# Layer 0 writes x1 transposed, with the x tile as the stationary operand, and layers 2 and 3 take their residual from an identity in the weights

## What is computed

```
x1 = x  + (own W0 of 8, 64x64, over the POSITIONS) . x + own bias, one value per position
x2 = x1 + down( silu(gate(x1)) * up(x1) )       gate, up: 512 -> 2048, down: 2048 -> 512,
                                                each with an own rank-16 adapter (A then B)
x3 = x2 + x2 . W2^T + scaled own rank-16 adapter        512 -> 512
y  = x3 + (own W3 of 200, 64x64, over the POSITIONS) . x3
```

## Time and profile before

| | us |
|---|---|
| median of the runs | 766.19 |
| the profiled execution's own time | 767.69 |
| its span in the trace | 765.9 |
| TensorE matmuls busy | 727.8 |
| VectorE busy | 601.1 |
| ScalarE busy | 284.8 |
| GpSimd busy | 255.3 |

### The profile page before, as it was taken

The page is one execution under the profiler, slowest core; times in us unless marked ns, Lnnn a source line. Parts: engine busy times, 40 slices in busy tenths (PEclk is TensorE's granted clock), DMA queues, the critical chain, the costliest instruction groups (busy, mean ns, idle before and its releaser), DMA issues.

```text
span 765.9 us, 10652 instructions
## 1 busy us (share of the span) xinstructions
PE 727.8 (95%) x3626; PEld 606.9 (79%) x3626; DVE 601.1 (78%) x1010; ACT 284.8 (37%) x508; POOL 255.3 (33%) x489
## 2 busy tenths in 40 slices
PE   6779889999999999989899999999999999899997
PEld 4547678888888888878778888888888888788886
DVE  7975768797878778799898979787888877766675
ACT  3445523333424333434353334242434333134232
POOL 4724231515223232350327162534425231241100
PEclk9979999999999999999999999999999999999999
DMA  7366520313212121203723232221212061212112
GB/s 209 87 81 194 164 80 29 104 37 108 83 56 83 55 84 56 83 27 111 248 59 109 71 103 73 70 86 58 89 55 85 28 192 32 79 29 70 42 55 83
DMA packets 65941, 66.02 MB, mean 86 GB/s; under 512 B 31712, under 2 KB 48096, under 8 KB 65888
## 3 DMA queue, kind: packets, MB, share of 16 engines
q1 hardware_dynamic: 57248, 45.92, 19.9%
q0 software_dynamic: 7296, 19.41, 8.7%
q10 hardware_dynamic: 1344, 0.02, 0.1%
HBM read 56.94 MB, written 8.39 MB: 85 GB/s over the span
## 4 chain that ended last, share of the span: by engine, by line
PE 84%; DVE 10%; issue 2%; ACT 2%; DMA 1%; POOLq 0%; POOL 0%; ACTq 0%; DVEq 0%
PE bank L1376 36%; PE bank L1474 22%; PE bank L1384 7%; PE bank L1633 6%; PE bank L1483 4%; PE bank L1622 2%; PE bank L1326 1%; PE bank L1599 1%; PE bank L1639 1%; DVE XC L882 1%; PE bank L1650 1%; PE bank L1611 1%; DVE hid L1001 1%; PE bank L1353 1%; DVE hs L1007 1%
## 5 line engine op out<-in xcount | busy, mean ns | idle before, releaser
L1376 PE MATMUL bank<-XC,WC 128*128 128x512 f32 x1344 | 332.9, 394 | 6.7 <-DVE tmp L975 2.2
L1376 PEld LDWEIGHTS bank<-XC,WC 128*128 128x128 f32 x1344 | 245.5, 190 | 54.8 <-issue 4.7
L1474 PE MATMUL bank<-wds,hs 128*128 128x512 f32 x768 | 187.6, 394 | 6.6 <-DVE X L1017 3.3
L1474 PEld LDWEIGHTS bank<-wds,hs 128*128 128x128 f32 x768 | 142.9, 190 | 35.8 <-DVE wds L960 3.8
L398 POOL DMA_INDIRECT BR<-in_L_cond_Bu_dram,boffs x64 | 71.9, 1124 | 265.7 <-DVE BL L954 251.1
L398 POOL DMA_INDIRECT BR<-in_L_cond_Bg_dram,boffs x64 | 76.1, 1189 | 95.2 <-DVE BL L954 80.2
L620 ACT ACTIVATE hs<-hid 128x512 fp32r<-128x512 f32 x64 | 40.3, 630 | 164.4 <-DVE hid L1001 111.4
L1017 DVE TENSOR_TENSOR X<-bank,X 128x512 f32<-128x512 f32 x128 | 86.5, 686 | 17.5 <-PE bank L1474 15.3
L614 ACT ACTIVATE hid<-hid 128x512 f32<-128x512 f32 x48 | 30.4, 633 | 148.4 <-DVE hid L984 75.9
L1384 PEld LDWEIGHTS bank<-UT,BL 128*128 128x128 f32 x512 | 76.4, 190 | 10.0 <-issue 2.1
L1384 PE MATMUL bank<-UT,BL 128*128 128x256 f32 x512 | 81.9, 283 | 1.3 <-ACT hid L611 1.3
(11 more groups left out here) (152 smaller groups left out, 827.9 us busy)
## 6 DMA issues: line engine op xcount, KB each, us to landing
RW<-in_L_cond_Wg_dram SPq DMA_DIRECT2D x16, 512.0 KB, 4.4
RW<-in_L_cond_Wu_dram SPq DMA_DIRECT2D x16, 512.0 KB, 5.1
RD<-in_L_cond_Wd_dram SPq DMA_DIRECT2D x16, 512.0 KB, 3.5
out_dram<-XR SPq DMA_DIRECT2D x16, 256.0 KB, 2.0
X<-in_x_dram SPq DMA_DIRECT2D x8, 256.0 KB, 6.2
udp<-in_x_dram SPq DMA_DIRECT2D x8, 256.0 KB, 4.5
x1park<-RD SPq DMA_DIRECT2D x8, 256.0 KB, 4.2
x2park<-X SPq DMA_DIRECT2D x8, 256.0 KB, 2.5
```

The source lines that it names most:

```text
L1376: last = nc.tensor.matmul(psum[:, :], WC[:, t, left, a, k, :], XC[:, right, b, k, :], start=(first and k == 0 and n == 0), stop=(k == 1 an ...
L1474: last = nc.tensor.matmul(psD[j % 2][:, :], hs[:, f, a, j * P:(j + 1) * P], wds[:, f, b, :], start=(f == 0 and n == 0), stop=(f == 1 and n ...
```

## The change

- `layer0(p)` now makes x1 transposed: four matmuls with one of the four strided slices of the x tile (`by_feature`, every fourth float) stationary and W0 plus identity moving (128 columns), then one matmul of 40 rows that adds the bias (`ones` against `bsel`). Four PSUM banks take turns. ScalarE's `xr_copy` is the only eviction. `x1_sum`, `x1_bias`, `transposes` and `add_identity` are gone; GpSimd adds the identity as it places W0.
- VectorE builds `bsel` (`bias_table`, `biases`). At the start it combines the first weights earlier.
- x1 of the two halves has its own buffers `XA` and `XB`, feature-major; the second half is parked from `XB`. `xin` has four buffers instead of two, two of them in `RD`. `load_d(0)` waits for the last `layer0` instead of the last transposes and parks.
- `down` is transposed as well: a strided slice of `wds` stationary, `hs` moving; `evict` adds to `XA`. `lora_down` is transposed too: 12 matmuls of 256 columns per duo instead of 6 of 512.
- x2 is feature-major, so `transposes2` is gone. VectorE adds the identity to W2 (`w2_identity`, end of unit 15) and to the W3 tables (`w3_identity`, end of unit 14); `x3_sum` and `y_sum` are gone. `x3_high` and `x3_low` read the PSUM bank of layer 2, and `layer2` of the next duo waits for `x3_low`. ScalarE copies y out (`y_out`), into four buffers instead of two.
- The last stretch's orders on TensorE, VectorE and ScalarE are rewritten accordingly. The warm-up is 24 matmuls of 128 columns instead of 5 of 256 and 5 of 128.

```diff
...
-    x1park = nc.dram_tensor("x1park", (HP, P, FEAT), f32).ap()
-    x2park = nc.dram_tensor("x2park", (HP, P, FEAT), f32).ap()
+    x1park = nc.dram_tensor("x1park", (P, KT, HT), f32).ap()
+    x2park = nc.dram_tensor("x2park", (P, KT, HT), f32).ap()
...
-        XR = sb("XR", [P, KT, HT])
-        X1 = sb("X1", [P, HP, FEAT])
+        XA = sb("XA", [P, KT, HT])
+        XB = sb("XB", [P, KT, HT])
...
+        xin = [udp[:, s * FEAT:(s + 1) * FEAT] for s in range(2)] + [RD[:, s, :] for s in range(2)]
...
+        def l0_bank(p):
+            return (psD[0], psD[1], psR[0], psR[1])[p % 4]
...
+        XT = [XB[:, n, :].rearrange("p (k t) -> p k t", k=2) for n in range(4)]
...
+        xc_raw = [dict(zip((B11, B21, B22), (blocks(XA)[0], blocks(XA)[1], blocks(XA)[3]))),
+                  {B11: XB11, B21: XB21, B22: XB22, T1: XB12, T2: XB11, T3: XB12, T4: XB21}]
+        xc_raw[0].update({T1: XT[0], T2: XT[1], T3: XT[2], T4: XT[3]})
...
+        def by_feature(v):
+
+            return v.rearrange("p (o k) -> p k o", k=KT)
...
+                    if p >= HP + XIN:
+                        sp.wait_ge(s_l0, p - XIN + 1)
+                    sp.dma_start(xin[p % XIN], x_pairs[p * P:(p + 1) * P, :]).then_inc(s_xin[p % XIN], 16)
 
                 def park_x1(p):
-                    sp.wait_ge(s_x1b, p - HP + 1)
-                    sp.dma_start(x1park[p - HP, :, :], x1s[p % 2]).then_inc(s_x1st[p % 2], 16)
+                    sp.wait_ge(s_xr, p + 1)
+                    at = slice((p - HP) * P, (p - HP + 1) * P)
+                    sp.dma_start(x1park[:, :, at], XB[:, :, at]).then_inc(s_x1st, 16)
...
-                        sp.wait_ge(s_tr, PAIRS)
-                        for s in range(2):
-                            sp.wait_ge(s_x1st[s], 16 * HP // 2)
+
+                        sp.wait_ge(s_l0, PAIRS)
...
+                for p in range(HP + XIN, PAIRS):
+                    load_xin(p)
+                    if p == HP + XIN + 1:
                         load_u(1)
                 load_d(0)
+                for p in range(HP, PAIRS):
+                    park_x1(p)
...
-                        last = nc.gpsimd.tensor_copy(w0bd_of(p)[rows, rows].rearrange("p (c f) -> p c f", f=KT),
-                                                     w0tab[rows, bass.ds(cols[half], RANK), :])
+
+                        last = nc.gpsimd.tensor_tensor(w0bd_of(p)[rows, rows].rearrange("p (c f) -> p c f", f=KT),
+                                                       w0tab[rows, bass.ds(cols[half], RANK), :],
+                                                       ident[rows, rows].rearrange("p (c f) -> p c f", f=KT), ALU.add)
...
-                def x1_bias(p):
-
+                def xr_copy(p):
                     act.wait_ge(s_l0, p + 1)
-                    if p == HP:
-                        act.wait_ge(s_x1, HP)
-                    if p >= HP + 2:
-                        act.wait_ge(s_tr, p - 1)
-                        act.wait_ge(s_x1st[p % 2], 16 * ((p - HP) // 2))
-                    nc.scalar.activation(x1_of(p), psD[p % 2][:, :], ACT.Identity, bias=bias[:, p:p + 1]).then_inc(s_x1b, 1)
-
-                def xr_copy(p):
-                    act.wait_ge(s_tr, p + 1)
                     if p >= HP:
                         act.wait_ge(s_xcl, 7)
                     at = p % HP * P
-                    nc.scalar.activation(XR[:, :, at:at + P], psR[p % 2][:, :].rearrange("p (k t) -> p k t", k=KT),
+                    nc.scalar.activation(XF[p // HP][:, :, at:at + P], l0_bank(p)[:, :].rearrange("p (k t) -> p k t", k=KT),
                                          ACT.Copy).then_inc(s_xr, 1)
...
+                def x3_high(d, q):
+                    act.wait_ge(c_l2, 2 * d + q + 1)
+                    if d >= 2:
+                        act.wait_ge(c_l3, 2 * (d - 2) + q + 1)
+                    nc.scalar.activation(x3s[d % 2][q][:, 0, :], psD[q][:, :], ACT.Copy).then_inc(c_x3h, 1)
...
+                def y_out(d, q):
+                    act.wait_ge(c_l3, 2 * d + q + 1)
+                    if d >= 2:
+                        act.wait_ge(c_out[d % 2][q], 16 * (d // 2))
+                    nc.scalar.activation(y[d % 2][q], psR[q][:, :], ACT.Copy).then_inc(c_y, 1)
...
+                def w2_identity():
+                    dve.wait_ge(s_w2ld, 16)
+                    for k in range(KT):
+                        own_block = w2_raw[:, k, k * P:(k + 1) * P]
+                        last = nc.vector.tensor_tensor(own_block, own_block, ident[:, :], ALU.add)
+                    last.then_inc(s_w2i, 1)
...
-                def x1_sum(p):
-                    dve.wait_ge(s_l0, p + 1)
-                    nc.vector.scalar_tensor_tensor(out=X1[:, p, :], in0=psD[p % 2][:, :], scalar=bias[:, p:p + 1],
-                                                   in1=X1[:, p, :], op0=ALU.add, op1=ALU.add).then_inc(s_x1, 1)
...
-                    nc.vector.tensor_tensor(X1[:, j, :], psD[j % 2][:, :], X1[:, j, :], ALU.add).then_inc(s_evict, 1)
+                    sums = XA[:, j % KT, j // KT * 512:(j // KT + 1) * 512]
+                    nc.vector.tensor_tensor(sums, psD[j % 2][:, :], sums, ALU.add).then_inc(s_evict, 1)
...
+                    if unit == ALL - 2:
+                        w3_identity(0)
+                        w3_identity(1)
+                    if unit == ALL - 1:
+                        w2_identity()
...
+                bias_table()
+                biases(0)
                 gather_rows()
-                biases()
...
                 move_matrices()
                 masks()
-                x1_sum(0)
-                x1_sum(1)
-                x1_sum(2)
-                g_combine(0)
-                x1_sum(3)
                 raw_low(G, 0)
-                x1_sum(4)
-                add_identity()
-                x1_sum(5)
-                x1_sum(6)
-                x1_sum(7)
                 xc_low(0, B11)
+                xc_low(0, B21)
+                sums_low(G, 0)
...
-                def x3_sum(d, q):
-                    dve.wait_ge(c_l2, 2 * d + q + 1)
-                    dve.wait_ge(s_x2, 2 * d + q + 1)
-                    if d >= 2:
-                        dve.wait_ge(c_y, 2 * d + q - 3)
-                    nc.vector.tensor_tensor(x3[d % 2][q], psD[q][:, :], x2_of(d, q), ALU.add).then_inc(c_x3, 1)
-
-                def y_sum(d, q):
-                    dve.wait_ge(c_l3, 2 * d + q + 1)
-                    if d >= 1:
-                        dve.wait_ge(c_out[q], 16 * d)
-                    nc.vector.tensor_tensor(y[q], psR[q][:, :], x3[d % 2][q], ALU.add).then_inc(c_y, 1)
...
                 for d in range(DUOS):
                     if d + 1 < DUOS:
+                        x2_sum(d + 1, 0)
+                        x2_sum(d + 1, 1)
                         xt_low(d + 1)
-                    x3_sum(d, 0)
-                    if d + 2 < DUOS:
-                        x2_sum(d + 2, 0)
-                        x2_sum(d + 2, 1)
-                    if d + 1 == DUOS:
-                        y_sum(d - 1, 0)
-                        x3_low(d, 0)
-                    x3_sum(d, 1)
+                    x3_low(d, 0)
+                    x3_low(d, 1)
                     if d + 1 < DUOS:
                         u2_mask(d + 1)
-                        if d >= 1:
-                            y_sum(d - 1, 0)
-                        x3_low(d, 0)
-                    if d >= 1:
-                        y_sum(d - 1, 1)
-                    x3_low(d, 1)
-                y_sum(DUOS - 1, 0)
-                y_sum(DUOS - 1, 1)
+                    w3_low(d, 0)
+                    w3_low(d, 1)
...
                 def layer0(p):
+
                     pe.wait_ge(s_w0c, p + 1)
                     if p < HP:
                         pe.wait_ge(s_xload[p], 16)
                     else:
-                        pe.wait_ge(s_xin[p % 2], 16 * ((p - HP) // 2 + 1))
-                    if p >= HP + 2:
-                        pe.wait_ge(s_x1b, p - HP - 1)
-                    elif p >= 2:
-                        pe.wait_ge(s_x1, p - 1)
-                    nc.tensor.matmul(psD[p % 2][:, :], w0bd_of(p), x_of(p), start=True, stop=True).then_inc(s_l0, 1)
-
-                def transposes(p):
-                    if p < HP:
-                        pe.wait_ge(s_x1, p + 1)
-                    else:
-                        pe.wait_ge(s_x1b, p - HP + 1)
-                    if p >= 2:
-                        pe.wait_ge(s_xr, p - 1)
+                        pe.wait_ge(s_xin[p % XIN], 16 * ((p - HP) // XIN + 1))
+                    if p >= 4:
+                        pe.wait_ge(s_xr, p - 3)
                     for k in range(KT):
-                        last = nc.tensor.transpose(psR[p % 2][:, k * P:(k + 1) * P],
-                                                   x1_of(p).rearrange("t (c k) -> t k c", k=KT)[:, k, :], ident[:, :])
-                    last.then_inc(s_tr, 1)
```

(54 more changed lines are left out.)

365 lines of the change are left out of this document (166 added, 199 removed).

## The result

The changed kernel takes 793.56 us (median of 4 runs, 793.33 to 793.96), the kernel before 766.39 in the same rounds (766.14 to 767.77). The ratio is 1.0351, 95% interval 1.0333 to 1.0369. I had forecast 750.6, with a range that ends at 758.5. The profiled execution has a span of 792.1 us against 765.9.

A forecast was written before the change was run, and what follows sets the result against it. Engine-alternating waits, mostly VectorE's, bound the start; TensorE bounds unit 0 and later, with short VectorE waits. Terms -3.0 - 4.4 - 1.1 + 0.3 - 7.4 = -15.6 from the 766.19 median gave 750.6 us, range 745.5 to 758.5.

The forecast's parts named there:

- The strided weight load: `down`'s 768 strided loads: stride lengthens a load but hardly its spacing, so cost nothing; ends 0 and 31 ns each.
- Bound D: Rival: strided loads not hidden in `down`, 258 ns set the pace, 23.4 us more, 774; chance 0.08.
- B: Rival: each strided load in `down` costs its extra 8.5 ns, 6.5 us in all, 757.1; chance 0.12.
- Layer 0 at the start: Start: first two pairs at half speed, then 1.2 us each, ScalarE limits; -3.0 us, ends 0 and 5 gained.
- rival C: Half the start and unit 0 gains swallowed (4.3 us), last stretch gives 5 instead of 7.4: 757.5; chance 0.15.
- Unit 0 and its end: Unit 0: cheaper pairs -1.0, waits gone -3.4, about -4.4; its end, VectorE's idle time won, about -1.1.
- The Wd transfer: End of unit 0: Wd loaded 5 us earlier, so its 3.44 us leave the chain; about -1.1 gained.
- Units 1 to 15 and the last stretch: Units +0.3 for `w3_identity`; last stretch -7.4, mainly transposes and waits removed, with `w2_identity` +0.9 and one new wait 0.5.
- wait for `x3_low`: Last stretch: `layer2` of the next duo waits for `x3_low`, hidden; wrong if TensorE waits for it in every duo.
- Two of the signs: Prediction wrong if `down` has more than 230 ns per matmul, or a layer 0 pair costs over 1.5 us.

The follow-up runs named there:

- all_flat: Changed kernel with contiguous slices in layer 0, `down` and `lora_down` at once (wrong features in each slice): 765.08 us, 0.9975 of the kernel before.
- after_xb: Changed kernel with only ScalarE's `idx_b` and `scal` transfers issued ahead of the bias wait and transfers: 792.06 us, 1.0337 of the kernel before.
- contig_warm_xb: contig plus 20 warm-up matmuls of 512 columns, x tiles 6 and 7 before tables A, `idx_b` and `scal` before bias transfers: 756.68 us (0.9864).
- step2_warm_xb: step2_warm plus x tiles 6 and 7 loaded before tables A, and `idx_b` and `scal` transfers issued before the bias transfers: 759.38 us (0.9907).
- contig: Changed kernel with features in blocks of 128, so slices are contiguous, and Wg, Wu, Ag, Au loaded to match; correct result: 766.52 us (0.9996).
- step2_warm: Changed kernel with slices of every second float, weights loaded to match, and 20 warm-up matmuls of 512 columns for 24 of 128: 761.63 us (0.9957).

## Why the prediction was wrong

**The strided weight load was the step that failed**, and it had a section of its own. I took nothing, with 31 ns as the upper end, from x1's transposes: loads of 208 against 140 ns with spacings of 117.5 against 109. It is worth 28.5 of the 43.0 us between forecast and result; the start gives 11.2 more (+8.2 instead of -3.0) and unit 0 3.1, both told below. An ordinary load pays more: 188 becomes 307 to 330. The transposes of `table` in the changed kernel, strided at step 4 too, still take what the x1 transposes took, as the rows of that line and of layer 0's say (ns, least, median, most):

```profile
L1572 PEld LDWEIGHTS bank<-ident,RW x16: 198/211/219, 673.2 to 682.3; 128*128 128x128 f32 x16
```

```profile
L1333 PEld LDWEIGHTS bank<-w0second,udp x32: 308/329/332, 62.3 to 87.7; 128*128 128x128 f32 x32
```

Both are strided float32 loads of 128 columns, so the row that I carried over measured another kind of load. What such a load does to the pace is nearly one number: strided loads follow each other every 233 (2.80/12) to 258 ns (2.06/8), contiguous ones every 119 (1.43/12) to 136 (1.09/8). With matmuls of 512 columns, 227.5 ns each, 64 groups of 12 lose (2.875 - 2.735) = 0.14 each, 9.0 us; with 256 columns a duo loses 1.37; with 128 a pair of unit 0 loses 0.91. I looked for the cost in `down` alone, the one place with room; `lora_down` went into the sum at 1.43 us a duo, the price of contiguous slices, and a pair of layer 0 at 0.94 for its eight matmuls, the spacing of the transposes. Bound D was the rival with this mechanism, at 774; its 23.4 us were too many for `down` (9.0 measured), and it left out the other two places (18.3). B's price of 8.5 ns in `down` was the nearest for that place (9.0 us over 768 loads are 11.7), and its 6.5 us are 22 short of the whole.

**Layer 0 at the start (-3.0, was +8.2 without stride).** I took two pairs at half speed because the kernel before has that the earlier trace rows. The changed kernel does all eight there, 2.72 us each in all_flat instead of 1.2, and W0 is 2.6 us late. I read the slow rows as a matter of the first 6 us and not of what TensorE does in them, as the timeline of the kernel before has it:

```profile
7.90 3.75 PE L1326 MATMUL bank<-X,hid 128*128 128x512 f32 x4 [4.31 <-POOL hid L387]
...
12.30 1.55 PE L1326 MATMUL bank<-X,hid 128*128 128x512 f32 x2
...
14.15 1.02 PE L1326 MATMUL bank<-X,hid 128*128 128x512 f32 x2
```

That kernel had a shorter warm-up (2.4 us against 5.4) and a longer wait (4.31 against 3.83), and was out of the low clock by its fourth pair, which took 1.02. It runs matmuls of 512 columns there, with transposes between. The changed kernel's eight pairs are matmuls of 128 columns and one of 512, and all eight are slow. The warm-up can't be all of it, then: the work of layer 0 itself differs. Which property of that work it is was not tested; the wide warm-up goes around the question, since TensorE enters layer 0 at the full clock and keeps it.

That the landing of W0 depends on ScalarE's transfers was in no row that I used; after_xb shows it. With both mended contig_warm_xb has -0.9 and step2_warm_xb -2.3, not -3.0: GpSimd's select of A takes over, which the sum put beside the rest, and with contig's eight pieces of A it ends another 1.4 later. This is what rival C said of the start and unit 0, waits in place of those removed and half of the first three terms lost: it put the loss at 4.3 us, contig_warm_xb has 5.1 (8.5 forecast, 3.4 measured), step2_warm_xb 3.9. Its other half, a last stretch of 5, didn't come, and its own numbers add up to 757.3, not 757.5.

**Unit 0 and its end (-5.5, was -2.4).** The wait for the x tile is gone, and a pair costs 1.32 to 1.52 us contiguous (contig_warm_xb), against 1.33 before and 1.2 forecast: where I had -1.0, the work itself lost about 0.7 (eight pairs at 1.42 against 1.33). Its eight matmuls are as forecast (0.89 to 1.09 us against 0.94); the bias matmul is not: I priced it at 0.23 from `layer2`'s matmuls, and it takes 0.43, as long as a float32 record of 512 columns does in the earlier trace rows. The Wd transfer left the chain as forecast, but VectorE's work at the end of the unit takes its place there, from 79.92 to 90.38 in contig_warm_xb with hardly a gap. Of the missing 3 us, 1.8 are the pairs (11.4 against 9.6); that the rest is VectorE's end of the unit is read from the chain and not tested.

**Units 1 to 15 and the last stretch (+1.2 and -8.3, were +0.9 and -8.4 without stride).** These were right as sums, each within 0.3: `w2_identity` took 0.81 where I had 0.9, the duos are 11.1 us apart, and no wait for `x3_low` appears. TensorE's wait for the split of W3 at the end is 1.8 us, against 1.2 before.

Two of the signs that I had named say it at once: `down` over 230 ns per matmul (235 and 244: 2.82 and 2.93 for 12) and a pair of layer 0 over 1.5 us (2.16 and 2.48).

## What to carry to other kernels

A duration in the trace is a price only for the same kind of operation: before you lean on it, ask whether it was a transpose or an ordinary matmul and how many columns stood behind it, and where it isn't the same, ask in every place that has such an operation what it would cost if nothing hid it. In these runs a float32 slice of 128 columns as stationary operand was free or nearly free at step 2, and at step 4 cost 106 to 121 ns per load with matmuls of 128 or 256 columns and 12 ns with matmuls of 512. A change at the start moves the clock and the landing of transfers too: look at what TensorE does, and how long it waits, ahead of the first real matmul and in the first layer itself, and read its clock from durations where the column may not have begun.

## What the runs showed of the hardware

- Two small transfers (`idx_b`, `scal`) that ScalarE issues ahead of the bias transfers and their wait, instead of behind, moved the landing of W0, issued by SyncE at the same time in both kernels, from 9.3 to 6.7 us. That is shown (after_xb); why is not, and the kernel before has 6.7 with these two behind the bias.
- With 24 narrow matmuls as warm-up and 2.0 us of waiting, TensorE stayed at 1.2 GHz for layer 0; with 20 wide ones and 2.1 us, it kept 2.4 in some executions and lost it in others; with 0.8 us or none it kept 2.4 in the profiles of step2_warm_xb and contig_warm_xb, and the 4 times of each lie within 1 us. Whether the narrow warm-up with no wait would do was not tried. The kernel before, with a wait of 4.3 us, left 1.2 GHz within its first pairs of 512-column matmuls; the changed kernel's matmuls still had it in the six of 512 columns behind layer 0 (2.93 us from 33.36 on; six of them later take 1.65).
- The column of the granted clock reads 1.00 at the start of each of these profiles, also where durations are those of 0.50 (all_flat from 10.44 to 32.3, against step2_warm from 13.84 on).
- In the same program a float32 load of 128 columns at step 4 takes 211 ns in a transpose and 329 in a matmul (medians). What makes the difference stays open.
